# An expert stage with its gathers, its result places and its bookkeeping rearranged: five token gathers ahead of the bias' weights, eight places for slot results, the far slots' work in parts

## The reference, cut to what matters

```
logits = xf @ gate_w.T
w, idx = jax.lax.top_k(logits, TOP_K)          # TOP_K = 2 of 32 experts
w = jax.nn.softmax(w, axis=-1)
combine = zeros((T, 32)).at[arange(T)[:, None], idx].add(w)
def body(acc, params):
    W, b, c = params
    return (acc + c[:, None] * (xf @ W.T + b), None)
out, _ = jax.lax.scan(body, zeros_like(xf), (expert_w, expert_b, combine.T))
x = x + tanh(g_ffn[1]) * out
```

## Time and profile before

| | us |
|---|---|
| median of 3 timed runs | 901.85 (899.71 to 902.27) |
| the profiled execution's own time | 906.39 |
| its span, first to last instruction | 904.6 |
| TensorE busy | 837.1 (93%) |
| VectorE busy | 654.6 (72%) |
| GpSimd busy | 424.2 (47%) |
| ScalarE busy | 397.4 (44%) |

### The profile page before, as it was taken

How to read it: one execution, slowest core, us unless ns; L and a number is a source line. 1 busy time by engine, 2 the same in 40 slices (tenths; PEclk the granted TensorE clock), 3 DMA queues, 4 the chain that set the end, 5 groups by cost and what they waited for, 6 DMA issues and landing times.

```text
span 904.6 us, 13117 instructions
## 1 busy us (share of the span) xinstructions
PE 837.1 (93%) x4337; PEld 700.3 (77%) x4337; DVE 654.6 (72%) x1300; ACT 397.4 (44%) x1009; POOL 424.2 (47%) x386
## 2 busy tenths in 40 slices
PE   5878999999999999999999999999999897989980
PEld 4666888888888888888888888878877686877860
DVE  4775878867778876787886778766852765999975
ACT  4634334324434423433523433444133535978970
POOL 5488447535527542734843644430020257765730
PEclk9989999999999999999999999999999968999995
DMA  8402101100200300110110120201152616999807
GB/s 328 164 1 94 70 1 59 59 1 23 94 3 5 111 0 0 46 70 1 59 57 0 46 93 1 94 12 54 47 187 85 244 63 213 346 337 331 313 37 280
DMA packets 23641, 91.13 MB, mean 101 GB/s; under 512 B 6576, under 2 KB 7088, under 8 KB 15776
## 3 DMA queue, kind: packets, MB, share of 16 engines
q1 hardware_dynamic: 17440, 81.00, 24.5%
q0 software_dynamic: 6144, 9.46, 2.9%
HBM read 86.23 MB, written 14.68 MB: 112 GB/s over the span
## 4 chain that ended last, share of the span: by engine, by line
PE 82%; DVE 7%; POOL 4%; DMA 2%; ACT 2%; issue 1%; SPq 0%; POOLq 0%; ACTq 0%; DVEq 0%
PE bank L145 23%; PE bank L147 22%; PE bank L146 22%; PE bank L1703 6%; PE bank L1710 3%; DVE cT_lo L1221 2%; PE bank L1610 1%; DVE x L1476 1%; PE bank L1551 1%; DMA raw_v<-in_wv 1%; PE bank L1516 1%; PE bank L139 1%; DMA last_xn<-xn_rows,place_token 1%; POOL qT L580 1%; PE bank L1534 1%
## 5 line engine op out<-in xcount | busy, mean ns | idle before, releaser
L580 POOL TENSOR_TENSOR qT<-straight,turned 128x512 f32<-128x512 f32 x64 | 82.6, 1291 | 147.5 <-DVE turned L1268 147.5
L884 ACT ACTIVATE probs<-bank,negmax 128x128 f32<-128x128 f32 x256 | 90.5, 366 | 129.3 <-DVE negmax L1279 129.3
L1268 DVE TENSOR_TENSOR turned<-bank,sinT 64x512 f32<-64x512 f32 x160 | 110.2, 689 | 2.2
L145 PE MATMUL bank<-xT_hi,wq_hi 128*128 128x512 f32 x256 | 106.1, 415 | 2.0 <-DVE xT_lo L121 2.0
L147 PE MATMUL bank<-xT_hi,wq_lo 128*128 128x512 f32 x256 | 102.3, 399 | 0.0
L145 PE MATMUL bank<-wo_hi,oT_hi 128*128 128x512 f32 x256 | 100.3, 392 | 2.0 <-POOL wo_lo L567 1.9
L146 PE MATMUL bank<-xT_lo,wq_hi 128*128 128x512 f32 x256 | 102.0, 398 | 0.0
L147 PE MATMUL bank<-wo_hi,oT_lo 128*128 128x512 f32 x256 | 100.2, 391 | 0.0
L146 PE MATMUL bank<-wo_lo,oT_hi 128*128 128x512 f32 x256 | 99.7, 390 | 0.0
L1221 DVE TENSOR_TENSOR cT_lo<-ring,cT_hi 128x1024 fp32r<-128x1024 f32 x72 | 87.6, 1219 | 12.6 <-ACT cT_hi L807 12.6
L891 ACT ACTIVATE pT_hi<-bank 128x512 fp32r<-128x512 f32 x64 | 38.2, 597 | 132.1 <-PE bank L1710 132.0
(11 more groups left out here) (223 smaller groups left out, 2046.3 us busy)
## 6 DMA issues: line engine op xcount, KB each, us to landing
ring<-in_ew SPq DMA_DIRECT2D x36, 1024.0 KB, 8.4
raw_big<-in_wq SPq DMA_DIRECT2D x9, 1024.0 KB, 4.8
raw_big<-in_wo SPq DMA_DIRECT2D x8, 1024.0 KB, 4.8
ring<-picked SPq DMA_DIRECT2D x8, 512.0 KB, 6.8
raw_k<-in_wk SPq DMA_DIRECT2D x8, 256.0 KB, 5.0
ctx_raw<-in_ctxT SPq DMA_DIRECT2D x4, 512.0 KB, 6.0
raw_v<-in_wv SPq DMA_DIRECT2D x8, 256.0 KB, 4.9
x<-in_x SPq DMA_DIRECT2D x2, 1024.0 KB, 11.4
```

The lines of the kernel that those rows point to most:

```text
L145: nc.tensor.matmul(out_, hi, r_hi, start=start, stop=False)
L580: nc.gpsimd.tensor_tensor(dst, straight[:, k, :], turned[:, k, :], ALU.add).then_inc(rope_sum, 1)
L884: ex = nc.scalar.activation(probs[:, u % 2, h, :], bank_scores[u % 2][:, h * S:(h + 1) * S], ACT.Exp, bias=negmax[:, u % UNITS, h:h + 1], ...
L1268: last = nc.vector.tensor_tensor(turned[dst, k, :], bank[src, :], sinT[src, tok], ALU.mult)
```

## The change

GpSimd issues the gathers of slots 0 to 4 ahead of `combine_weights` (`AHEAD` is 5; they were two). The bias' turns and products move one slot back (`COMB` is 3). The results get eight places, four in `loaded` as before and four in `late_results` over memory that is free by then; the banks of TensorE stay four (`BANKS`). Six semaphores become shared ones, to make room for the four of the new places, and the waits on them count higher. VectorE's far-slot work is cut up: the sixteen small comparisons of `owners` become one operation at slot 10 and the rest of it follows at slot 11; the six operations of `far_slots` go one each to slots 12 to 17; `at_far` is written in sixteen parts, one after each of slots 10 to 16, two after 17 to 20 and one after 21. `far_rows` moves from slot 14 to 22, `write_rows` from 15 to 23.

```diff
-        LANES = 4
-        ALWAYS = NX + LANES
+        LANES = 8
+        BANKS = 4
+        ALWAYS = NX + 4
         RING = 9
-        COMB = 2
+        COMB = 3
+        AHEAD = 5
...
-        result = loaded
+        late_results = over("qT", "late_results", [P, LANES // 2, E], F32, 8192)
...
+        def result(lane):
+            return loaded[:, lane, :] if lane < LANES // 2 else late_results[:, lane - LANES // 2, :]
+
         def bank_of(k):
-            return psum[(6, 7, 4, 2)[k % LANES]][:, :]
+            return psum[(6, 7, 4, 2)[k % BANKS]][:, :]
...
-                sp.dma_start(gw[:, :, :], a["gw"]).then_inc(g_gate, 16)
+                sp.dma_start(gw[:, :, :], a["gw"]).then_inc(m_in, 16)
...
-                pool.wait_ge(m_in, 32)
+                pool.wait_ge(m_in, 48)
...
                 pool.wait_ge(tokens_ready, 1)
-                take(0)
-                take(1)
+                for k in range(AHEAD):
+                    take(k)
                 combine_weights()
-                for k in range(2, TAKEN):
+                for k in range(AHEAD, TAKEN):
                     take(k)
...
-                def far_slots():
+                def far_slot_of_pairs(part):
 
                     pairs = [P, NB * TOP, NX]
                     ready()
-                    step(nc.vector.tensor_tensor(far_weighted[:, :, :], onehot[:, :, :, :].bitcast(F32).rearrange("p t k e -> p (t k) e"),
-                                                 first_far[:, :].unsqueeze(1).broadcast_to(pairs), ALU.mult))
+                    if part == 0:
+                        step(nc.vector.tensor_tensor(far_weighted[:, :, :], onehot[:, :, :, :].bitcast(F32).rearrange("p t k e -> p (t k) e"),
+                                                     first_far[:, :].unsqueeze(1).broadcast_to(pairs), ALU.mult))
+                    elif part == 1:
+                        step(nc.vector.tensor_reduce(far_slot[:, :], far_weighted[:, :, :], AX.X, ALU.add))
...
+                def far_places(pair):
+
+                    nc.vector.tensor_scalar(at_far[:, pair, :], numbers[:, :], rest[:, pair:pair + 1], None, ALU.is_equal).then_inc(far_at, 1)
+
+                def mark_slot(pair):
+
+                    return 10 + pair if pair < 7 else 17 + (pair - 7) // 2
+
+                def owners_passed():
                     ready()
...
-                def far_places(half):
-                    pairs = slice(half * NB, half * NB + NB)
-                    nc.vector.tensor_tensor(at_far[:, pairs, :], numbers[:, :].unsqueeze(1).broadcast_to([P, NB, P]),
-                                            rest[:, pairs].unsqueeze(2).broadcast_to([P, NB, P]), ALU.is_equal).then_inc(far_at, 1)
+                    step(nc.vector.tensor_tensor(passed[:, :, :], summed_to.unsqueeze(1).broadcast_to([P, 16, NX]),
+                                                 numbers[:, 0:16].unsqueeze(2).broadcast_to([P, 16, NX]), ALU.is_le))
 
                 def owners():
-                    for j in range(16):
-                        last = nc.vector.tensor_scalar(passed[:, j, :], summed_to, float(j), None, ALU.is_le)
-                    step(last)
...
                     if k == 10:
-                        far_slots()
-                    if k in (11, 12):
-                        far_places(k - 11)
-                    if k == 15:
+                        owners_passed()
+                    if k == 11:
+                        owners()
+                    if 12 <= k < 18:
+                        far_slot_of_pairs(k - 12)
+                    for pair in range(NB * TOP):
+                        if mark_slot(pair) == k:
+                            far_places(pair)
+                    if k == 23:
                         dve.wait_ge(far_laid, 1)
                         write_rows(slice(NX, SLOTS), psum[3][:, 0:EXTRA], 1)
-                    if k == 16:
-                        owners()
...
-                    pe.wait_ge(far_at, 2)
+                    pe.wait_ge(far_at, NB * TOP)
...
-                    after(pe, e_kept, k - LANES + 1)
+                    after(pe, e_kept, k - BANKS + 1)
...
-                    if k == 14:
+                    if k == 22:
                         far_rows()
```

More of the change, by code:

```diff
@@ L355, in program @@
             sem(f"r_{n}") for n in ("exp", "sum", "inv", "wts", "comb", "combT", "combk", "bias", "added"))
[L356 to L357 removed]
+        m_in, constants, exact, m_step, far_counted, far_built, far_at, far_laid, rows_ready, tokens_ready, owners_ready, m_out = (
+            sem(n) for n in ("m_in", "constants", "exact", "m_step", "far_counted", "far_built", "far_at", "far_laid",
                              "rows_ready", "tokens_ready", "owners_ready", "m_out"))
@@ L488, in _ @@
                 sp.wait_ge(g_mm, 2 * KC)
-                sp.dma_start(c_raw[:, :, :], a["ctx"]).then_inc(g_ctx, 16)
+                sp.dma_start(c_raw[:, :, :], a["ctx"]).then_inc(f_words, 16)
                 sp.wait_ge(f_added, NB)
-                sp.dma_start(before_raw[:, :], a["before"]).then_inc(m_const, 16)
+                sp.dma_start(before_raw[:, :], a["before"]).then_inc(f_small, 16)
                 for n in range(3):
-                    sp.dma_start(eb_raw[n * NX:(n + 1) * NX, :], a["eb"]).then_inc(m_const, 16)
+                    sp.dma_start(eb_raw[n * NX:(n + 1) * NX, :], a["eb"]).then_inc(f_small, 16)
                 early(2)
@@ L704, in give @@
                     pool.indirect_dma_start(out=picked, out_offset=bass.IndirectOffsetOnAxis(ap=place_row[:, k:k + 1].bitcast(U32), axis=0),
-                                            in_=result[:, lane, :], in_offset=None, bounds_check=TOP * T - 1, oob_is_err=False).then_inc(y_out[lane], 16)
+                                            in_=result(lane), in_offset=None, bounds_check=TOP * T - 1, oob_is_err=False).then_inc(y_out[lane], 16)
                 weights_rest(1, range(KC))
@@ L812, in keep_result @@
                     after(act, y_out[lane], 16 * (k // LANES))
-                    nc.scalar.activation(result[:, lane, :], bank_of(k), ACT.Copy).then_inc(e_kept, 1)
+                    nc.scalar.activation(result(lane), bank_of(k), ACT.Copy).then_inc(e_kept, 1)
                 def one(k, end):
@@ L1198, in far_places @@
-                def far_places(half):
-                    pairs = slice(half * NB, half * NB + NB)
-                    nc.vector.tensor_tensor(at_far[:, pairs, :], numbers[:, :].unsqueeze(1).broadcast_to([P, NB, P]),
-                                            rest[:, pairs].unsqueeze(2).broadcast_to([P, NB, P]), ALU.is_equal).then_inc(far_at, 1)
+                    if part == 0:
[3 more added lines that the diff above has]
+                        step(nc.vector.tensor_reduce(far_slot[:, :], far_weighted[:, :, :], AX.X, ALU.add))
+                    elif part == 2:
+                        step(nc.vector.tensor_tensor(far_slot[:, :], far_slot[:, :], full[:, :], ALU.add))
+                    elif part == 3:
+                        step(nc.vector.scalar_tensor_tensor(far_slot[:, :], full[:, :], 0.0, far_slot[:, :], ALU.is_gt, ALU.mult))
+                    elif part == 4:
+                        step(nc.vector.tensor_tensor(in_far[:, :, :], numbers[:, 1:17].unsqueeze(1).broadcast_to([P, NB * TOP, 16]),
+                                                     far_slot[:, :].unsqueeze(2).broadcast_to([P, NB * TOP, 16]), ALU.is_equal))
+                    else:
+                        nc.vector.tensor_tensor(far_code[:, :, :], in_far[:, :, :],
+                                                pair_codes[:, :, :].rearrange("p t k -> p (t k)").unsqueeze(2).broadcast_to([P, NB * TOP, 16]),
+                                                ALU.mult).then_inc(far_built, 1)
@@ L1418, in _ @@
                 softmax_scale(0)
-                dve.wait_ge(m_in, 32)
+                dve.wait_ge(m_in, 48)
                 attended(0)
```

25 lines of the change are left out of this document (6 added, 19 removed).

## The result

The changed kernel takes 895.14 us (median of 20 runs, 892.41 to 900.6), the kernel before in the same session 901.66 (20 runs): a ratio of 0.9934, 95% interval 0.9916 to 0.9952. That is 6.5 us faster, inside the range of the forecast and 2 us short of its 8.4.

What follows compares the result with a forecast made beforehand. TensorE was taken to bound the kernel, idling at slot 1's gather and behind VectorE in slots 10 to 19. 8.33 - 0.4 + 0.5 = 8.4 us off the median of 901.85 gives 893.4 us, range 890 to 898.

Steps and rivals of the forecast that it cites:

- The front: Slots 0 to 9: five early gathers remove slot 1's wait and slow clock, so slot 10 starts 8.33 us earlier.
- rival (c): Slot 2's gather was late for a reason other than its issue, slot 1 starts as now: 901 to 902; chance 0.07.
- Slot 5's gather: At the start of slot 4: this gather, issued behind combine, lands up to 0.8 us late; 0.4 us booked as lost.
- rival (a): The wait moves to slot 5's gather, landing 8.5 to 10 us after issue: 896 to 899; chance 0.22.
- (d): Combine on GpSimd takes far longer, TensorE holds at slots 3 and 4: 904.8 if it takes 16 us; chance 0.05.
- The far work: Slots 10 to 23: cutting up VectorE's far-slot work leaves an excess of 6.50 against 7.05 us, 0.5 gained.
- marks at 0.19: VectorE's sixteen writes of `at_far`, 128 columns each, were taken to cost 0.19 us apiece, bounds 0.11 and 0.28.
- the wait of 1.33 us at `far_rows`: At slot 22 the far products wait on TensorE for the second half of the weights (1.14) and the last mark (0.19).
- Rival (b): Far work hides better: marks at 0.11, no wait at slot 22, no loss at slot 4: 891.0; chance 0.16.
- What costs nothing: Eight result places gain nothing, as ScalarE's copies wait for products; shared semaphores and the earlier `owners` cost nothing.
- the second part: Far-slot work spread over twelve slots from slot 10: 0.5 us gained, a loss of 0.8 with marks at 0.28.
- a slow clock after slot 0: Sign of being wrong: TensorE's granted clock low anywhere past slot 0; no size given.

Runs made afterwards that it cites:

- e2: Kernel before with the far work in parts alone (two gathers ahead, four result places); 903.73 us, ratio 1.0021.
- e3: Changed kernel with four result places instead of eight; 900.27 us, ratio to the kernel before 1.0001.
- e8: Changed kernel with the bias' weights worked out on VectorE in four parts, bias products from slot 4; 895.5 us, ratio to the kernel before 0.9942.
- e9: Changed kernel with the bias' weights on VectorE, done by slot 1, bias products from slot 3; 893.46 us, ratio to the kernel before 0.9912.
- e6: Changed kernel with the far work in bursts as before, its products at slot 14; 896.85 us, ratio to the kernel before 0.9939.
- e7: Kernel before with eight result places alone; 902.88 us, ratio 1.0021.
- e4: Changed kernel run again unaltered for a second profile; 894.76 us, ratio to the kernel before 0.9949.
- e10: e9 with the far slots' products at slot 23 instead of 22; 891.49 us, ratio to the kernel before 0.9886.

## Why the prediction was right, and where it was not

**The front.** Measured from `turn(0)`, slot 1 starts at 4.91 us, forecast 747.4 - 742.51 = 4.89, and slot 10 at 36.87 instead of 44.61: 7.74 earlier, where 8.33 - 0.4 was forecast. Gathers issued earlier were the cure, at full clock, as worked out; rival (c) is out.

**Slot 5's gather.** Combine took 747.67 - 740.69 = 6.98 us, forecast 6.13 + 1.14 = 7.27 with bounds of 6.1 and 8.4, and the turn that opens slot 4 waits 0.17 where 0.4 was booked: the gather is there 754.05 - 747.67 = 6.38 us after its issue, forecast 6.5. The median of 6.7 us that rival (a) leaned on the earlier trace rows takes in eight stores at 2.0 us; the gathers alone have 8.2 in the kernel before. Rivals (a) and (d) are out. The trace shows the two engines hold each other up in the other direction too: while combine's product of 512 columns ran on GpSimd, from 742.13 to 743.18, a subtraction on VectorE took 1.75 us against the usual 1.22:

```profile
742.52 1.75 DVE L1231 TENSOR_TENSOR cT_lo<-ring,cT_hi 128x1024 fp32r<-128x1024 f32 x1
```

This agrees with the Trainium skill, page "SBUF — State Buffer", section "SBUF: two separate sides", by which a VectorE operation with two SBUF inputs and a GpSimd operation that reads SBUF lock each other out.

**The far work.** Slots 10 to 23 take 52.33 us, forecast 52.28, with marks at 0.19. But the sum is right by a trade, and that is luck: the wait of 1.33 us at `far_rows` did not come, since late gathers held TensorE back by 1.33 just before. Rival (b) had named this, no wait because TensorE gets there late itself, but its gain did not follow, since the lateness cost as much. In the kernels with these products at slot 22 and no late gather the forecast wait is there: 1.16 us in e2, 1.18 in e3, 1.20 in e8, 1.17 in e9. What the parts are worth could not be told from nothing (e6 beside the changed kernel); 0.5 us is too small for these intervals.

**The step that failed** is "What costs nothing": eight places were said to gain nothing. By e3 and e7 they are worth nothing without the early gathers and the whole gain with them. The prediction named the condition, GpSimd four slots behind, and did not work out whether it would hold. It could have: combine was forecast to end at 751.8, and four gathers 1.31 apart follow, those of slots 5 to 8, so the first scatter starts at about 757.0. The scatters of the kernel before landed a median of 7.9 us after their issue, by this row of its view of transfers (target and source, queue, count, median us from issue to landing):

```profile
picked<-loaded,place_row POOLq DMA_INDIRECT x36, 7.9
```

That gives 764.9. Slot 4 was forecast to start at 757.49; its copy comes at its end, near 761.0, and with four places needs the one that this scatter empties: 3.9 us late. e3 measured 4.44 at that copy, and slots 5 and 6 together took 6.5 us more than two bias slots, the slow clock included. The row that I leaned on, 28 copies waiting for products only the earlier trace rows, is of a kernel whose TensorE stood still for 5.7 us at slot 1 and so gave GpSimd time. With four places in the change, most of the forecast gain would have gone, as in e3. The time came out right because the change holds the eight places too.

**The size.** The stage shortened by 8.6 us in the first pair of profiles and by 161.8 - 155.1 = 6.7 in the second; the medians differ by 6.5, and by 6.1 for e4. Forecast were 8.4. The front held in both: slots 0 to 9 are 7.74 us shorter in the first pair and 44.59 - 36.83 = 7.76 in the second. What varies is the second part: slots 10 to 23 are 0.50 shorter in the first pair (52.83 against 52.33), as forecast, and 0.93 longer in the second (52.90 against 53.83). The slow clock of e4's slot 22 costs 1.85 us, about the size of what is missing, and no term of the sum held it, though the prediction had a slow clock after slot 0 among its signs of being wrong. The parts alone show the same spread: with the wait at `far_rows` at full clock slots 10 to 23 take 51.91 us (e3), with a slow clock behind the same wait 53.09 (e2). How often the clock falls in the runs without a profile no view shows, so that share stays open.

## What to carry to other kernels

When an issue is moved forward on an in-order queue, ask which work on that queue does not move: the consumer now runs ahead of it, and the number of buffers between them must cover the new distance. A row that shows no wait holds only for the pace at which it was taken. Where an engine is full over many slots, a wait that is removed can come back at the next point where its results are read (e8, e9); look there too, and move that reader (e10).

## What the runs showed of the hardware that was not expected

TensorE's granted clock fell to about half after a short wait in some executions and not in others. The far slots' products at slot 22 waited 1.16 us in e2, 1.18 in e3, 1.20 in e8 and 1.17 in e9. Behind them the clock fell to 0.50 in e2 (from about 830 to 833.5 us) and e8 (from 821.7 to 825) and stayed at 1.00 in e3 and e9; the slot lasted 7.97 and 7.83 us against 6.40 and 6.36, so a fall cost some 1.5 us. In e4 it fell in the same slot behind a wait of 0.15 us. Which waits bring it down these runs don't settle.

GpSimd's issue of a gather took 1.00 us ahead of the experts' slots in both kernels (739.57 in the earlier trace rows, 739.66 in the changed kernel). In the bias slots it took longer. In the kernel before a gather and a scatter there look like this:

```profile
768.49 1.44 POOL L696 DMA_INDIRECT last_xn<-xn_rows,place_token  x1 [0.31 <-issue]
770.73 1.03 POOL L704 DMA_INDIRECT picked<-loaded,place_row  x1 [0.79 <-PE bank L1610]
```

and in the changed kernel like this:

```profile
767.35 1.52 POOL L700 DMA_INDIRECT last_xn<-xn_rows,place_token  x1 [0.30 <-issue]
769.18 1.44 POOL L708 DMA_INDIRECT picked<-late_results,place_row  x1 [0.30 <-ACT late_results L817]
```

Before, GpSimd still idled 0.8 us ahead of a scatter. Now the pair makes some 3.55 us without a break, as long as a bias slot, so GpSimd didn't catch up its three slots there. VectorE is nearly always busy in either stretch (15.28 of 16.00 us from 760 to 776 before, 64.75 of 66.00 from 750 to 816 in the changed kernel); what makes the issues longer was not tested.

The landings of gathers grew to 15.2 us (16.1 in e8) in a stage whose DMA share is about 1.0 in many windows, 1.01 and 1.02 in those shown for e4 and the changed kernel. This fits transfers that queue behind the weights' loads, and was not tested by itself; in e6, with the same gathers and places, the longest took 10.8.
